# Attention's maxima split, output bias and part of the band factor moved to GpSimd and ScalarE; PE's pieces of a batch placed anew; MoE gathers issued one tile further ahead

## The reference, cut to what matters

```
x = x + attn(ln(x))                 # causal, 16 heads of 16, rotary positions
x = x + xattn(ln(x), ctx, ctx)      # "cross": 120 keys, biases on q, k, v and the output (bo)
x = x + peer_ffn(ln(x))             # untouched by the change
x = x + attn(ln(x))                 # "band": scores + 0.1 where |i-j| <= 2, biases, bo
x = x + bidaf(ln(x), ctx)           # attention between two sequences
x = x + moe(ln(x))                  # 8 experts, top 2, hidden 1024

scores = einsum('bhqd,bhkd->bhqk', Q, K) / sqrt(d)
attn   = softmax(scores); out = (attn @ V) @ Wo.T + bo
# moe: topk_idx = top_k(softmax(x @ Wr + br), 2); out = sum over e of gate_e * (relu(x W1_e + b1_e) W2_e + b2_e)
```

## Time and profile before

| | us |
|---|---|
| median of 3 runs (lowest, highest) | 4071.61 (4066.42, 4080.31) |
| the profiled execution's own time | 4071.27 |
| its span, first to last instruction | 4069.5 |
| causal, about 26 to 515 | 490 |
| cross, about 520 to 930 | 410 |
| peer, about 930 to 2600 | 1670 |
| band, about 2600 to 3110 | 510 |
| bidaf, about 3110 to 3390 | 280 |
| moe, 3390 to 4069.5 | 680 |

### The profile page before, as it was taken

How to read it: one execution, slowest core, us unless ns; L and a number is a source line. 1 busy time by engine, 2 the same in 40 slices (tenths; PEclk the granted TensorE clock), 3 DMA queues, 4 the chain that set the end, 5 groups by cost and what they waited for, 6 DMA issues and landing times. The chain is left out here.

```text
span 4069.5 us, 98588 instructions
## 1 busy us (share of the span) xinstructions
PE 3425.7 (84%) x33488; PEld 2849.1 (70%) x33489; DVE 2980.0 (73%) x11747; ACT 1109.9 (27%) x2400; POOL 1658.6 (41%) x1626
## 2 busy tenths in 40 slices
PE   6999858784899988889999999777786886799998
PEld 4777635444788888888888888555554666688887
DVE  6778646667999999999999999499995444433332
ACT  1333424442222222222222222154442111122221
POOL 3223122212666666666666667532320000233332
PEclk8999968876999999999999999899997886799999
DMA  5344344432000000000000000244441005466665
GB/s 148 100 113 106 82 112 111 112 83 93 2 2 3 2 2 2 2 2 2 2 2 2 2 2 2 65 107 104 107 105 32 7 7 173 131 168 168 169 171 130
DMA packets 256580, 278.71 MB, mean 68 GB/s; under 512 B 43841, under 2 KB 200641, under 8 KB 255713
## 3 DMA queue, kind: packets, MB, share of 16 engines
q1 hardware_dynamic: 242401, 254.81, 22.1%
q0 software_dynamic: 13824, 19.18, 3.1%
HBM read 188.88 MB, written 72.42 MB: 64 GB/s over the span
## 5 line engine op out<-in xcount | busy, mean ns | idle before, releaser
L1129 POOL TENSOR_TENSOR peer_hot_v<-peer_hot_e,peer_parts 80x512 bf16<-80x512 bf16 x768 | 1038.1, 1378 | 505.0 <-DVE peer_hot_e L1168 504.1
L974 PE MATMUL peer_ps_u<-peer_up,peer_g 128*128 128x256 f32 x2048 | 547.9, 416 | 0.6 <-DVE x_all L1285 0.6
L955 PEld LDWEIGHTS peer_ps_h<-peer_xnT,peer_down 128*128 128x128 f32 x4096 | 511.6, 197 | 15.6
L955 PE MATMUL peer_ps_h<-peer_xnT,peer_down 128*128 128x128 f32 x4096 | 510.1, 279 | 0.0
L965 PE MATMUL peer_ps_w<-peer_hot_v,peer_hot_u 80*128 80x32 bf16 x12288 | 347.7, 177 | 177.1 <-DVE peer_g L1180 94.1
L965 PEld LDWEIGHTS peer_ps_w<-peer_hot_v,peer_hot_u 80*128 80x128 bf16 x12288 | 335.3, 97 | 204.0 <-DVE peer_hot_u L1172 109.4
L974 PEld LDWEIGHTS peer_ps_u<-peer_up,peer_g 128*128 128x128 f32 x2048 | 407.8, 208 | 55.6 <-issue 1.0
L1052 ACT ACTIVATE peer_g<-peer_ps_h 128x512 f32<-128x512 f32 x256 | 152.9, 597 | 901.9 <-PE peer_ps_h L955 901.9
L1172 DVE TENSOR_TENSOR peer_hot_u<-peer_count,peer_uvT 80x2048 bf16<-80x2048 bf16 x256 | 344.8, 1347 | 0.0
L1940 PE MATMUL moe_ps_t<-moe_xgT,moe_w 128*128 128x128 f32 x2304 | 275.3, 278 | 0.0
L1998 POOL DMA_INDIRECT moe_xg<-moe_xn_rows,moe_source x72 | 71.5, 993 | 485.7 <-DVE moe_target L2099 451.2
(11 more groups left out here) (353 smaller groups left out, 6874.2 us busy)
## 6 DMA issues: line engine op xcount, KB each, us to landing
moe_w<-in_moe_w SPq DMA_DIRECT2D x144, 512.0 KB, 4.9
causal_qs<-causal_qscratch SPq DMA_DIRECT2D x32, 384.0 KB, 3.8
cross_qs<-cross_qscratch SPq DMA_DIRECT2D x32, 384.0 KB, 3.6
band_qs<-band_qscratch SPq DMA_DIRECT2D x32, 384.0 KB, 3.9
moe_w<-in_moe_w SPq DMA_DIRECT2D x8, 1024.0 KB, 9.5
causal_qscratch<-causal_part SPq DMA_DIRECT2D x32, 192.0 KB, 2.0
causal_kscratch<-causal_part SPq DMA_DIRECT2D x32, 192.0 KB, 2.0
causal_ks<-causal_kscratch SPq DMA_DIRECT2D x32, 192.0 KB, 4.3
```

Source lines behind the costliest of these rows:

```text
L955: mm = nc.tensor.matmul(ps_h[:, n % 2, k * P:(k + 1) * P], down[:, c, 4 * n + k, :], xnT[:, par, c, :], start=(c == 0), stop=(c == DC - 1))
L974: mm = nc.tensor.matmul(ps_u[:], g[:, par, v, :], up[:, v, :], start=(v == 0), stop=(v == EV - 1))
L1129: ins = nc.gpsimd.tensor_tensor(hot_v[0:SEL, n % RING, part], hot_e[0:SEL, n % RING], w, ALU.mult)
```

## The change

In attention, for all three kinds:

- `turn_max`: ACT copies the transposed maxima from PSUM, once as fp32 (`nfull`) and once as bf16; POOL makes the middle and low part with three subtractions. DVE has no share in it.
- `PROJECT` is (2, 5, 8, 11) instead of (2, 4, 6, 8), `OUT` 13 for 10, `VALUES` 15 for 12, `weigh` is one step later, `sums` in step 4 for 2, `normalise` 7 for 5; `norm` runs a batch further ahead, in step 4; `moments` a macro later.
- The output bias is added to `x_all` by POOL beforehand (`bias`), and `out` on DVE is one instruction for both tiles.
- In band POOL does the factor of the even heads, DVE that of the odd ones. `probT` holds 16 heads instead of 8.
- The semaphore of the parts' writes is one for each chunk, so `stack` waits for its own chunk alone.

In bidaf SP writes finished rows of `x_all` to `out` during the loop. In moe `xn` has four buffers, W2 is loaded behind all of them, only four tiles of `x_all` are written there; the one-hot rounds are 16 of five instructions; `JT` is 71 instead of 72; ACT copies the gates beside the transposed rows, so that a gather needs only that copy, and gather(j+4) stands ahead of scatter(j).

```diff
-        PROJECT, OUT, VALUES, STACK = (2, 4, 6, 8), 10, 12, 10
-        NORMALISE = 5
+        PROJECT, OUT, VALUES, STACK = (2, 5, 8, 11), 13, 15, 10
+        WEIGH, SUMS, NORMALISE, MOMENTS, NORM = 6, 4, 7, 3, 4
...
-                    settle(parts_out, OUTS * (b + 1))
+                    settle(parts_out[c], OUTS * (b + 1))
...
+                def turn_max(self, b, par, c):
+                    act.wait_ge(nt_done, 2 * b + c + 1)
+                    wait(act, n_ready, 2 * b + c - 1)
+                    wait(act, n_out, 16 * (2 * b + c - 1))
+                    nc.scalar.activation(nfull[:, c, :], ps_n[0:CH, 0:S], ACT.Copy)
+                    nc.scalar.activation(npart[:, c, 0, :], ps_n[0:CH, 0:S], ACT.Copy).then_inc(n_taken, 1)
...
+                def factor(self, b, par, h):
+                    if kind != "band" or h % 2 == 1:
+                        return
+
+                    pool.wait_ge(p_ready, HEADS * b + h + 1)
+                    for k in range(KT):
+                        lo, hi = near[k]
+                        e = probT[:, h, kcol[k] + lo:kcol[k] + hi]
+                        ins = nc.gpsimd.tensor_tensor(e, e, band[:, k, lo:hi], ALU.mult)
+                    ins.then_inc(b_ready[0], 1)
+
+                def bias(self, b):
+                    if rope:
+                        return
+                    pool.wait_ge(xn_ready, b + 1)
+                    xt = x_all[:, bass.ds(b * TT, TT), :] if not isinstance(b, int) else x_all[:, b * TT:(b + 1) * TT, :]
+                    nc.gpsimd.tensor_tensor(xt, xt, bo[:].unsqueeze(1).broadcast_to((P, TT, D)), ALU.add).then_inc(biased, 1)
+
+                def turn_max(self, b, par, c):
+                    src, (high, middle, low) = nfull[:, c, :], (npart[:, c, k, :] for k in range(3))
+                    pool.wait_ge(n_taken, 2 * b + c + 1)
+                    wait(pool, n_ready, 2 * b + c)
+                    nc.gpsimd.tensor_tensor(nrest[:], src, high, ALU.subtract)
+                    nc.gpsimd.tensor_tensor(middle, src, high, ALU.subtract).then_inc(n_rest, 1)
...
-                    for t in range(TT):
-                        src = ps_p[:, 0, t * D:(t + 1) * D]
-                        if not rope:
-                            steps.link(nc.vector.tensor_tensor(ytmp[:, t, :], src, bo[:], ALU.add))
-                            src = ytmp[:, t, :]
-                        xt = x_all[:, b * TT + t, :]
-                        ins = nc.vector.tensor_tensor(xt, src, xt, ALU.add)
-                    ins.then_inc(y_used, 1)
+                    xt = x_all[:, bass.ds(b * TT, TT), :] if not isinstance(b, int) else x_all[:, b * TT:(b + 1) * TT, :]
+                    nc.vector.tensor_tensor(xt, ps_p[:, 0, :].rearrange("p (t c) -> p t c", t=TT), xt, ALU.add).then_inc(y_used, 1)
...
-JT += JT % 2
...
+                    wait(act, gate_ready, 2 * i + par - 1)
+                    nc.scalar.activation(xgT[:, par].rearrange("p c q -> p (c q)"), ps_x[:, 0:D], ACT.Copy)
+                    nc.scalar.activation(gates[:, par, :], xg[:, par, D:ROW], ACT.Copy).then_inc(xgt_used, 1)
...
             def gather(j):
-                wait(pool, xgt_done, j - 1)
-                wait(pool, gate_ready, j - 1)
+                wait(pool, xgt_used, j - 1)
...
-            for j in range(3):
+            for j in range(4):
                 gather(j)
             pool.wait_ge(x_out, 16)
             for j in range(JT):
-                if j + 3 < JT:
-                    gather(j + 3)
+                if j + 4 < JT:
+                    gather(j + 4)
                 scatter(j)
...
+            for n in range(NHOT):
+                wait(dve, hot_used, n - 1)
+                few = slice(n * HOTS // TOPE, (n + 1) * HOTS // TOPE)
+                nc.vector.tensor_tensor(rowhot[:, n % 2], iota16[:].unsqueeze(1).broadcast_to((P, HOTS, P)),
+                                        rowb[:, few, :].rearrange("p t k -> p (t k)").unsqueeze(2).broadcast_to((P, HOTS, P)),
+                                        ALU.is_equal)
```

More of the change, by code:

```diff
@@ L282, in macro @@
                         e.normalise(b - 1, 1 - par)
-                if s % 4 == 1 and s > 1:
-                    e.weigh(b, par, s // 4 - 1)
+                if s >= WEIGH and s % 4 == WEIGH % 4:
+                    e.weigh(b, par, (s - WEIGH) // 4)
+                if s == NORM and there(b + 3):
+                    e.norm(b + 3)
                 if there(b + 2):
-                    if s == 0:
-                        e.norm(b + 2)
                     if s == 1:
                         e.turn(b + 2, par)
+                    if s == 2:
+                        e.bias(b + 2)
                     if s in PROJECT:
@@ L1855, in _ @@
                 sp.wait_ge(xn_ready, g + 1)
-                sp.dma_start(rows[:, group, 0:D], xn[:, g % 2]).then_inc(xn_out[g % 2], 16)
+                sp.dma_start(rows[:, group, 0:D], xn[:, g % XN]).then_inc(xn_out[g % XN], 16)
+            tail = slice(TILES - NS * TT, TILES)
+            sp.dma_start(tiles_of(out[0:TOKENS, :])[:, tail, :], x_all[:, tail, :]).then_inc(x_out, 16)
+            for g in range(G):
                 sp.dma_start(w2[:, g:g + 1], w2_in[:, g:g + 1]).then_inc(weights, 16)
```

167 lines of the change are left out of this document (97 added, 70 removed).

## The result

| | before | after |
|---|---|---|
| median (lowest to highest), us | 4074.1 (4066.4 to 4080.3) | 4005.7 (4004.6 to 4017.7) |
| span of the profiled execution | 4069.5 | 4002.7 |
| causal | 509.3 | 516.7 |
| cross | 411.3 | 428.2 |
| peer (not changed) | 1668.4 | 1665.1 |

A forecast was written before the change was run, and what follows sets the result against it. Bounds taken: PE in causal, a chain in cross, DVE in band, the gather chain in MoE. Terms -40 - 10 - 5 + 13 - 6 - 45 = -93 from 4071.3 gave 3978 us, range 3895 to 4043.

The forecast's parts named there:

- MoE tiles: MoE's tile loop: the wait for the gather goes, tiles 7.25 us apart, 518 us against 558, -40 us.
- Tables: MoE's one-hot tables: 16 rounds of four take 23.7 us where 64 single rounds took 33.4 to 34, -10 us.
- Router: MoE's router: four xn buffers take out waits of about 5 us, -5 us (0 to -19).
- Cross: Cross attention: longer chain from turn to find, about 1.0 given back, net +0.9 us a batch, +13 us (-10 to +30).
- Causal: Causal attention: the stall stays 0.5 and only the wait for xn goes, -6 us (-15 to +10).
- Band: Band attention: DVE relieved, period 26.5 us a batch, -45 us (-85 to 0).
- Rival 1: Attention: the chain through POOL costs as much as DVE gave, band stays at 28.9, 4043 us; chance 0.10.
- Rival 2: Band: POOL becomes the bound, held up by DVE's pairs, band 33 us a batch, 4116 us, slower; chance 0.06.
- Rival 3: Attention: the chain hides and the clock stays high, band 23.5 us a batch, 3896 us in all; chance 0.16.
- Rival 4: MoE tiles: W1 at 7.6 us a tile holds them, not the gathers; MoE -35, 3998 us; chance 0.12.
- DVE beside POOL: Band: DVE's eight remaining factor pairs and POOL lock each other out, 5.8 us more, DVE 26 instead of 20.
- The sign for cross: Cross attention: find in step 0 would wait for the stack's DMA over 3 us instead of 2.

The follow-up runs named there:

- e6: The changed kernel with MoE's gathers issued three tiles ahead again instead of four; 4031 us, ratio to before 0.991.
- e7: The changed kernel with two xn buffers in MoE's router instead of four; 4004 us.
- e2: The changed kernel with attention's norm in step 10 instead of step 4; 3975 us, ratio to before 0.977.
- e12: The changed kernel with stack in step 7, norm in step 10, maxima's split on DVE and out in step 14 instead of 13; 3988 us, ratio 0.980.
- e10: The changed kernel with the maxima's split and all band factors back on DVE; 3998 us, ratio to before 0.983.
- e3: The changed kernel with the maxima's split back on DVE, without ACT and POOL; 3974 us, ratio to before 0.976.
- e8: The changed kernel with SP's stack in step 7, ahead of the maxima, and norm in step 10; 3939 us, ratio to before 0.970.
- e5: The changed kernel with the band factor of all heads back on DVE; 4006 us, ratio to before 0.986.
- e9: The changed kernel with the third projection in step 7 instead of step 8; 3997 us.
- e11: The changed kernel with stack in step 7, norm in step 10 and the maxima's split back on DVE; 3946 us, ratio to before 0.971.

## Why the prediction was right or wrong

The total, the sign and the range held. The mechanism held in MoE's tiles and in both chains of attention; of attention's gain about a quarter came, and the total is near because MoE is most of it and because peer and bidaf happened to be 7 us shorter. Of its terms:

- **MoE tiles, -40**: the stretch from the first W1 to the end of the last W2 in the chain went from 558.2 to 512.4 us, -46 (the last tile's W2, 3.4 us, lies behind it in both kernels). The wait is gone and the pace is 7.25, as forecast. The 518 counted the first and the last tile in full; of the first only W1 (5.3 us) lies in the stretch. e6 divides the gain: 31 us for the place of the gather, about 8 for the 72nd tile that is no longer there, and the rest, 7.78 to 7.70 us a tile, is left for the earlier release of the gathered rows; no run took that alone.
- **Tables, -10**: a round of four measured 1.71 us against 1.48 forecast, 16 x 1.71 = 27.4 against 33.4, so -6. The term that was too small is the 142-column instruction: 0.28 apart (1.11 for four), not 0.22. A part of that was arithmetic: 512 columns in 0.69 us are 1.35 ns each, and the working used 1.2.
- **Router, -5**: +2, outside its bounds of 0 to -19. The buffers were to take out waits of about 5 us; PE's waits were 1.8 us in all, and they are gone with two buffers too (e7). The rest is the clock, which the bounds took to be no worse than before: in the profiled execution it was at half throughout, and PE's busy time rose from 36.1 to 40.4 us.
- **Cross, +13**: +17 (1.7 us a batch and not 0.9). The chain was drawn rightly: from the turn to `find` the mean of nine batches went from 9.95 to 11.4 us, where 9.9 to 11.8 was forecast. The step that failed is that the other half would give back about 1.0: it went from 12.1 to 12.4 us. What is missing is step 4. In e2, with `norm` out of it, that half takes 11.1 us, which is the forecast's 1.0 less, and the chain's half is as long as before that edit. The prediction looked at DVE's sum of work and at the chain of the maxima, but not at what now stands next to what on DVE's queue.
- **Causal, -6**: +7, the wrong sign (the range reached to +10). The step that failed is "the stall stays 0.5, and only the wait for `xn` goes". The stack's stall went altogether, and the same meeting in step 4 took its place: e2 gives 0.57 of the 0.8 us back. By halves: `find` comes 12.9 us after the turn, as drawn (12.7), and the other half fell by 2.0 us, in e2 by 2.6. What is left of the loss, 0.2 us a batch, was not settled; PE also waits some 0.5 us at `out` for DVE's evacuation, and e12, which took that wait away, lost more than it saved.
- **Band, -45**: -34, a period of 27.3 where 26.5 was forecast. The loads of DVE and POOL were forecast within 1 us (20.9 and 20.3), PE's is 23.2 at a clock of 0.95, as it was before, and not the 21 to 22 of the full clock; the chain was forecast within 0.9: send-off at 5.4 us and `find` at 12.9 after the turn, where the working gives 6.2 and 13.8. The other half takes 14.4, near the upper end of the 11.5 to 14.5 that it had for a clock that stays up or falls. The term that was sized wrong is the choice of 26.5 between 24.8 and 28.7. But the reason given for the gain, the work that leaves DVE, was mostly wrong: e10, with the factor and the maxima on DVE, has 31 of the 34 us, and the maxima's move, counted as relief, cost 2.3 us a batch (e3).
- **Rival 1** (the chain costs as much as DVE gave) is what happened between e3 and the changed kernel, at 2.3 us a batch; it took nearly half of the gain and not all. **Rival 2** (POOL the bound) did not come: POOL is busy 74%. **Rival 3** needed the stack out of the way first; e8 comes nearest to it (cross 399, band 454, 3939 us). **Rival 4** fell with e6.
- **DVE beside POOL.** The factor's instruction went from a mean of 354 ns to 434 in the changed kernel's loop, and to 404 in e5, where POOL has no factor; POOL's own took 462. Half as many of them: 16 x 0.08 = 1.3 us a batch, where 5.8 were priced by the pairs of 1.20. That DVE's two-input instructions and POOL's hold each other up is stated by the Trainium skill (SBUF — State Buffer, Who interferes with whom); these means agree with the direction, and the 1.20 pair was the worst case and not the mean. How busy POOL is does not set the price by itself: between 2780 and 2990 us the mean is 375 ns in e3 (POOL busy 68%) and 341 in e10 (36%), but 566 in e9 and 494 in e6, whose band code is that of the changed kernel (430 in that stretch), with POOL busy 74 to 75% in all three.
- **The sign for cross.** The prediction looked for a wait of `find` for the stack of over 3 us instead of 2. It was 2.7 on average (21.8 in eight), against 1.9 (17.5 in nine).

## What to carry to other kernels

When pieces of work get new places, lay the changed order of each in-order queue out and look for long instructions that now stand next to each other: here two numbers that both became 4 cost 30 us, and no sum of loads showed it. An item that waits for a round trip through DRAM (the maxima on SP) should have nothing behind it that could have gone first: moving the stack ahead of it gave 50 us, where the whole change brought attention 10 (7.3 + 17.0 - 34.3). And relief for an engine is worth something only until the chain next to it is the longer; the factor's move was worth 2.6 us a batch alone and 0.3 to 0.8 beside the maxima's.

## What the runs showed of the hardware

bidaf took 269 to 276 us in ten kernels and 287 to 289 in four (e3, e10, e11, e12), the four that put the maxima back on DVE. Its code is the same in all thirteen changed kernels; the kernel before, which has the maxima on DVE too and no stores in bidaf, took 276. PE's instructions are the same in all; the clock is not. The busy time of the whole stage in the changed kernel:

```profile
3099.00:3371.70 272.70, 223.19 (x1088) 175.12 (x1088) 118.85 (x394) 52.07 (x165) 0.00 (x0) 0.86 0.08 25
```

And in e10:

```profile
3090.00:3378.60 288.60, 241.64 (x1088) 187.84 (x1088) 118.78 (x394) 52.70 (x165) 0.00 (x0) 0.79 0.08 24
```

The same 1088 matmuls took PE 18 us more at a mean of 0.79. There is one trace of each kernel, so whether the edit in the stage before decides it, or it falls out anew in each execution, is not shown, and 16 us are as much as many an edit is worth. The router showed the same on a smaller scale: with the same code and no gap on PE its 192 matmuls took 34.2 us in one kernel, 37.2 in seven and 40.4 in four. So a small gain in the total should be read stage by stage before it is believed.
